# Windowed attention with the values made once per token, masks in 32-row tiles, and attention outputs brought back by plain transposes

## The reference, cut to what matters

```python
mod = (silu(c) @ wmod).reshape(8, 6, 1, -1)        # sa, ca, ga, sb, cb, gb per sequence
h = layernorm(x) * (1 + ca) + sa
q, k, v = split(h @ w_qkv)                         # 16 heads of 8 columns
# windows of W = 64 tokens: a query sees its own window up to itself, and the whole window before
kcat, vcat = concat([k_prev, k_cur]), concat([v_prev, v_cur])   # 128 keys; window 0 has no k_prev
attn = softmax(where(causal & valid, q @ kcat.T / 8 ** 0.5, -inf))
x = x + ga * ((attn @ vcat) @ w_out)
h = layernorm(x) * (1 + cb) + sb
# 8 experts of 352 hidden columns, the best 2 per token, weights by a softmax over both scores
x = x + gb * moe(h)
```

## Time and profile before

| | |
|---|---|
| median of 3 executions | 282.27 us (280.81, 282.27, 283.45) |
| the profiled execution's own time | 282.76 us |
| its span, first to last instruction | 280.7 us |
| mean granted TensorE clock | 0.92 of full speed |
| busy: PE, PEld, DVE, ACT, POOL | 221.5, 150.3, 171.0, 115.3, 128.6 us |
| stages in the span | loads and first scores to about 25 us, attention to about 147, experts to about 256, final sum to the end |

### The profile page before, as it was taken

One profiled execution on the slowest core, in us unless ns is written; L12 is line 12 of the kernel. 1 busy time (PEld: TensorE's weight loads), 2 busy tenths in 40 slices (PEclk: granted clock), 3 DMA queues, 4 the chain that ended last, 5 costly groups with the idle time before them and its releaser, 6 DMA issues.

```text
span 280.7 us, 7719 instructions
## 1 busy us (share of the span) xinstructions
PE 221.5 (79%) x2694; PEld 150.3 (54%) x2695; DVE 171.0 (61%) x527; ACT 115.3 (41%) x259; POOL 128.6 (46%) x127
## 2 busy tenths in 40 slices
PE   8559589998999999998867893877999999994000
PEld 3315245565756656574545572655777777773000
DVE  2665869899697685869491773624244444443492
ACT  4213255555546564545253441223444444443330
POOL 8450626251828557392505165714344444445251
PEclk9957799999999999999997999879999999999555
DMA  6479400000100000010102021222221111100751
GB/s 166 121 292 456 200 2 2 2 2 4 31 12 22 21 22 21 8 34 2 41 2 57 28 59 49 61 90 50 66 59 55 48 55 46 56 30 30 236 169 44
DMA packets 16488, 19.32 MB, mean 69 GB/s; under 512 B 2578, under 2 KB 14998, under 8 KB 16202
## 3 DMA queue, kind: packets, MB, share of 16 engines
q1 hardware_dynamic: 13786, 14.43, 16.4%
q0 software_dynamic: 2240, 4.28, 4.3%
q10 hardware_dynamic: 432, 0.20, 0.3%
HBM read 13.03 MB, written 6.13 MB: 68 GB/s over the span
## 4 chain that ended last, share of the span: by engine, by line
PE 58%; DVE 16%; ACT 7%; DMA 5%; issue 4%; POOL 4%; another core or an unknown queue 2%; SPq 1%; ACTq 0%; DVEq 0%; POOLq 0%
PE pair L742 8%; PE pair L716 7%; PE pair L718 7%; PE pair L557 6%; PE pair L501 4%; PE pair L536 4%; ACT pt L826 4%; PE pair L724 4%; DVE nd L996 3%; PE pair L542 3%; PE pair L572 2%; DVE fin_b L1314 2%; PE pair L474 2%; PE pair L735 2%
## 5 line engine op out<-in xcount | busy, mean ns | idle before, releaser
L1422 POOL DMA_INDIRECT ranked<-y_sb,ix_u x36 | 35.3, 980 | 47.4 <-ACT y_sb L916 36.8
L1290 DVE TENSOR_TENSOR gated<-pair,act 128x352 f32<-128x352 f32 x36 | 18.9, 525 | 51.5 <-PE pair L718 40.2
L826 ACT ACTIVATE pt<-pair 128x1024 f32<-128x1024 f32 x32 | 33.0, 1031 | 27.3 <-PE pair L542 27.3
L996 DVE TENSOR_REDUCE nd<-pair 128x8 f32<-128x1024 f32 x32 | 37.7, 1220 | 10.7 <-PE pair L501 10.7
L1375 POOL DMA_INDIRECT routed<-pay,row_u x32 | 32.2, 1005 | 13.7 <-issue 6.3
L716 PE MATMUL pair<-we_sb,x_t 128*128 x72 | 29.8, 497 | 3.1 <-ACT x_t L910 3.1
L742 PE MATMUL pair<-we_sb,gated_t 128*128 x216 | 31.6, 284 | 0.8 <-ACT y_sb L916 0.8
L742 PEld LDWEIGHTS pair<-we_sb,gated_t 128*128 128x128 f32 x216 | 27.9, 197 | 1.6 <-issue 1.2
L718 PE MATMUL pair<-we_sb,x_t 128*128 x72 | 28.3, 476 | 0.0
L1342 POOL TENSOR_TENSOR rstd<-veps,cf_sb 128x2 f32<-128x2 f32 x8 | 6.0, 748 | 46.8 <-DVE veps L1036 46.8
L501 PE MATMUL pair<-km,q_sb 32*64 32x512 f32 x256 | 20.5, 700 | 4.3 <-POOL km L1364 2.2
(11 more groups left out here) (164 smaller groups left out, 399.9 us busy)
## 6 DMA issues: line engine op xcount, KB each, us to landing
we_sb<-we SPq DMA_DIRECT2D x1, 4352.0 KB, 18.6
xt_in<-routed SPq DMA_DIRECT2D x36, 64.5 KB
mod_bc<-mod_rows SPq DMA_DIRECT2D x1, 2048.0 KB, 7.8
fin_y<-ranked SPq DMA_DIRECT2D x8, 256.0 KB, 4.5
out<-fin_b SPq DMA_DIRECT2D x8, 128.0 KB, 1.8
x_all<-x SPq DMA_DIRECT2D x1, 896.0 KB, 6.8
ranked<-y_sb,ix_u POOLq DMA_INDIRECT x36
routed<-pay,row_u POOLq DMA_INDIRECT x32
```

What stands on the lines that cost most here:

```text
L826: act.activation(pt[:, 2 * half:2 * half + 2, :].rearrange("p j k -> p (j k)"), src[:, :], ACT.Exp).then_inc(done, 1)
L996: dve.tensor_reduce(nd[:, :, 2 * half:2 * half + 2, 0].rearrange("p s j -> p j s"), src[:, :].rearrange("p (j s k) -> p j s k", j=2, s=4), ...
L1290: dve.tensor_tensor(gated[n][:, 0:HID], H3_BANK[n][:, 0:HID], act1[n][:, :], ALU.mult).then_inc(gated_ready, 1)
L1422: pool.indirect_dma_start(ranked[:, :], bass.IndirectOffsetOnAxis(ap=ix_u[q][:, 0:1], axis=0), y_sb[q][:, :], None, bounds_check=TOPK * TO ...
```

## The change

- `project_v` makes V once per token: two matmuls of 128 tokens, 256 columns of M1. h_t loses its 64 zero columns and their memset. `copy_v` copies V in three pieces: all 128 rows of a tile to the odd chunk; rows 0 to 63 to the even chunk, as current keys; rows 64 to 127 of tile 0 to chunk 2, as previous keys.
- So in even chunks the current keys stand first, on partitions 0 to 63, and the previous ones on 64 to 127. In `scores_t` the even chunk's matmul is split into two of 64 output rows. POOL zeroes the ones of chunk 0 on partitions 64 to 127.
- The masks come from a small tile `late32` (the triangle's first 32 rows over 64 columns, and rows 32 to 63 over the last 32 columns), held four times, for each group of 32 partitions; 8 small DMAs load it, ahead of the large load of x. In `scores` 16 mask matmuls with 32x32 tiles take the place of 8; in `scores_t` 8 with 32x64 and 8 with 32x32 tiles, of 128 columns each, take the place of 4, now for both chunks apart.
- `output_t` makes four plain transposes, 512 columns of M0; `perm_o` goes, with its wait and its two POOL copies. `divide_output` picks outputs and denominators by its access pattern, with as many elements as before.
- `gate` moves ahead of `project_v`, and into M1 behind V (column 272; Z1 for the leftover period). DVE reads its scores by `read_gate` ahead of `divide_output`. New waits: `read_gate` for `v_copied` (the bank is read by ACT too) and for `hot1_ready` of the batch before; `neg_max_t` in period0, and the expert stage's step 2, for `sc8_ready`.

```diff
@@ sync
             sp.dma_start(cb_sb[:, :], cb[:, 0:CB_USED]).then_inc(ld_b, 16)
+            la = CB["late"][0]
+            for j in range(4):
+                sp.dma_start(late32[32 * j:32 * j + 32, 0:W], cb[0:32, la:la + W]).then_inc(ld_b, 16)
+                sp.dma_start(late32[32 * j:32 * j + 32, W:W + 32], cb[32:64, la + 32:la + W]).then_inc(ld_b, 16)
             sp.dma_start(x_all[:, 2:NT, :], xv[:, 2:NT, :]).then_inc(ld_x, 16)
@@ tensor, project_v
-                for c in range(4):
-                    last = mm(M1[:, c * P:(c + 1) * P], h_t[:, c * W:c * W + 2 * W], wqkv_sb[:, 2 * D:3 * D],
+                for t in range(2):
+                    last = mm(M1[:, t * P:(t + 1) * P], h_t[:, t * P:(t + 1) * P], wqkv_sb[:, 2 * D:3 * D],
                               start=True, stop=True)
@@ scores
-                for n in range(2):
-                    for a in range(2):
-                        for i in range(2):
-                            sv = S_BANKS[2 * i + n].rearrange("p (s k) -> p s k", s=4)
-                            mm(half(sv, a)[:, :, W:2 * W], half(ident_b, i)[:, 64 * i:64 * i + 64],
-                               half(late, i).unsqueeze(1).to_broadcast([W, 4, W]), start=True, stop=False,
-                               skip_group_check=True)
+                late = late32[:, 0:W].unsqueeze(1).to_broadcast([P, 4, W])
+                later = late32[:, W:W + 32].unsqueeze(1).to_broadcast([P, 4, 32])
+                for a in range(2):
+                    for j in range(4):
+                        sv = S_BANKS[j].rearrange("p (s k) -> p s k", s=4)
+                        one = group(ident_b, j)[:, 32 * j:32 * j + 32]
+                        mm(sv[64 * a:64 * a + 32, :, W:2 * W], one, group(late, j), start=True, stop=False,
+                           skip_group_check=True)
+                        mm(sv[64 * a + 32:64 * a + 64, :, W + 32:2 * W], one, group(later, j), start=True, stop=False,
+                           skip_group_check=True)
@@ scores_t
                     for j in range(4):
-                        fv = F_BANKS[j].rearrange("p (s q) -> p s q", s=4)
-                        mm(fv[:, :, a * W:(a + 1) * W], group(k_sb[par], j)[:, c * W:c * W + 2 * W],
-                           group(qm[par], j)[:, :, c * W:(c + 1) * W], start=False, stop=False, skip_group_check=True)
-                for n in range(2):
-                    for i in range(2):
-                        fv = F_BANKS[2 * i + n].rearrange("p (s q) -> p s q", s=8)
-                        one = half(ident_b, i)[:, 64 * i:64 * i + 64].unsqueeze(1).to_broadcast([W, 8, W])
-                        last = mm(half(fv, 1), half(late, i), one, start=False, stop=True, skip_group_check=True)
+                        fv = F_BANKS[j].rearrange("p (s q) -> p s q", s=4)[:, :, a * W:(a + 1) * W]
+                        for low, keys in ((0, 2 * W),) if a else ((0, W), (W, W)):
+                            at = c * W + (W - low if a == 0 else 0)
+                            mm(fv[low:low + keys], group(k_sb[par], j)[:, at:at + keys],
+                               group(qm[par], j)[:, :, c * W:(c + 1) * W], start=False, stop=False,
+                               skip_group_check=True)
+                for a in range(2):
+                    for j in range(4):
+                        one = group(ident_b, j)[:, 32 * j:32 * j + 32].unsqueeze(1).to_broadcast([32, 4, 32])
+                        fv = F_BANKS[j].rearrange("p (s q) -> p s q", s=4)[:, :, a * W:(a + 1) * W]
+                        mm(fv[64 * a:64 * a + 64, :, 0:32], group(late32, j)[:, 0:W], one, start=False, stop=False,
+                           skip_group_check=True)
+                for a in range(2):
+                    for j in range(4):
...
+                        last = mm(fv[64 * a + 32:64 * a + 64, :, 32:64], group(late32, j)[:, W:W + 32], one,
+                                  start=False, stop=True, skip_group_check=True)
@@ output_t
-                        at = (2 * p + r) * RCOLS
-                        last = mm(M0[:, at:at + RCOLS], o_sb[:, p, r, :], perm_o[:, :], start=True, stop=True,
-                                  skip_group_check=True)
+                        at = (2 * p + r) * P
+                        last = pe.transpose(M0[:, at:at + P], o_sb[:, p, r, :], ident)
@@ tensor, period0
+                if b < B:
+                    pe.wait_ge(negt_ready, 2 * b + 1)
+                if b >= 2:
+                    gate(b - 2, M1 if b < B else Z1)
                 if b + 1 < B:
-                    pe.wait_ge(negt_ready, 2 * b + 1)
                     project_v()
...
-                    gate(b - 2, M0)
...
+                    if b >= 2:
+                        pe.wait_ge(sc8_ready, b - 1)
                     neg_max_t(2 * b + 1)
@@ scalar, copy_v
-                act.copy(v_lane[b % 2][:, :, HD:2 * HD],
-                         M1.rearrange("p (h e) -> p h e", e=HD)).then_inc(v_copied, 1)
+                to = v_lane[b % 2][:, :, HD:2 * HD].rearrange("p (t n h) e -> p t n h e", t=2, n=2)
+                v = M1[:, 0:2 * P].rearrange("p (t h e) -> p t h e", t=2, e=HD)
+                act.copy(to[:, :, 1, :, :], v)
+                act.copy(to[0:W, :, 0, :, :], v[0:W])
+                act.copy(to[W:2 * W, 1, 0, :, :], v[W:2 * W, 0, :, :]).then_inc(v_copied, 1)
@@ vector
-                rv = M0[:, 0:4 * RCOLS].rearrange("p (x c) -> p x c", c=RCOLS)
-                dve.reciprocal(rden[:, :, :], rv[:, :, 64:RCOLS]).then_inc(sums_inverted, 1)
+                rv = M0.rearrange("p (x k d) -> p x k d", k=4, d=HD)
+                dve.reciprocal(rden[:, :, :], rv[:, :, 2:4, 0]).then_inc(sums_inverted, 1)
...
+            def read_gate(e, m):
                 dve.wait_ge(gate_done, e + 1)
+                if e + 4 <= B:
+                    dve.wait_ge(v_copied, e + 4)
+                if e >= 1:
+                    dve.wait_ge(hot1_ready, e)
                 dve.tensor_copy(sc8[:, :, :].rearrange("p a e -> p (a e)"),
                                 m[:, GATE_AT:GATE_AT + 2 * E]).then_inc(sc8_ready, 1)
...
@@ vector, period0
+                if b >= 2:
+                    read_gate(b - 2, M1 if b < B else Z1)
                 if b >= 1:
                     divide_output(b - 1)
                 if b >= 2:
-                    choose_experts(b - 2, M0)
+                    choose_experts(b - 2)
```

More of the change, by code:

```diff
@@ L40 @@
 G = 2 * B
-RCOLS = 72
 CF = {}
@@ L60 @@
 N_CB = _columns(CB, [("ident", P), ("before", P), ("ones", P), ("region", E), ("late", 4 * W), ("none", 4 * W)])
-CB_USED = CB["late"][0] + W
+CB_USED = CB["late"][0]
 def build(nc, x, c_t, wqkv, wout, wmod, wg_t, we, cf, cr, cb, out):
@@ L104, in build @@
         quadmask = sb("quadmask", [P, 4])
-        perm_o = sb("perm_o", [P, RCOLS])
         x_all = sb("x_all", [P, NT, D])
@@ L112, in build @@
         normed = sb("normed", [P, 2, D])
-        h_t = sb("h_t", [P, WIN])
+        h_t = sb("h_t", [P, S])
         q_sb = sb("q_sb", [P, S])
@@ L193, in build @@
         ones_b = cb_("ones")
-        late = cb_sb[:, CB["late"][0]:CB["late"][0] + W]
         nd_high = nd[:, :, :, :].rearrange("p s j i -> p (s j i)").bitcast(BF16).rearrange(
@@ L200, in group @@
             return t[32 * j:32 * j + 32]
-        def half(t, i):
-            return t[64 * i:64 * i + 64]
         def mod(b, which):
@@ L500, in scores @@
                     for j in range(4):
-                        last = mm(half(S_BANKS[j], a), group(q_sb, j)[:, c * W:c * W + W],
+                        last = mm(S_BANKS[j][64 * a:64 * a + 64, :], group(q_sb, j)[:, c * W:c * W + W],
                                   group(km[par], j)[:, :, c * W:c * W + 2 * W], start=False, stop=True,
@@ L803, in modulate @@
                     act.wait_ge(v_done, b)
-                act.activation(h_t[:, W:WIN], M0[:, 0:S], ACT.Identity, bias=mod_t[:, B + b:B + b + 1],
+                act.activation(h_t[:, :], M0[:, 0:S], ACT.Identity, bias=mod_t[:, B + b:B + b + 1],
                                scale=mod_t[:, b:b + 1]).then_inc(ht_ready, 1)
@@ L1256, in aside @@
                 if i == 5 and at == "b":
-                    choose_experts(B - 1, XT_BANK)
+                    read_gate(B - 1, XT_BANK)
+                    choose_experts(B - 1)
                 if i == 6:
```

35 lines of the change are left out of this document (15 added, 20 removed).

## The result

The changed kernel took **286.34 us** (median of four runs), the kernel before 282.61 us beside it (four): a ratio of **1.014, 95% interval 1.009 to 1.019**. The forecast was 280.3, its range ended at 284.2. The profiled execution has a span of 284.1 us against 280.7.

A forecast was written before the change was run, and what follows sets the result against it. PE's chain was taken to bound the kernel, with held PE signals setting negt's start in batches 3 to 6. Middle batches -1.96, batches 0 to 2 +0.33, last batch -0.34: sum -1.97, forecast 280.3 us, range 276.6 to 284.2.

The forecast's parts named there:

- V once: In project_v, two matmuls for four take four of eight passes off PE: 0.45 us less per batch.
- Transposes: In output_t, four transposed tiles take 0.44 us in place of 0.93: 0.48 less per batch.
- scores_t: Split product and new masks in scores_t: 1.74 us against 1.63, +0.11 for each of 16.
- two ends: Bounds for scores_t: -0.25 us if changing tile columns alone costs nothing, +0.5 if tiles don't run side by side or reloads add up.
- The middle batches, -1.96: Four batches that scatter while attending: negt follows the exponential unheld, -0.60, second scores_t +0.11; -0.49 us each.
- wrong from the root: Stated failure condition: output_t's two signals fall into a GpSimd issue's tail again, or x's load holds DVE over 0.3 us.
- Rival C: Middle batches gain nothing: the hold falls on whatever PE signals next, negt starts as before; +0.4, 282.7 us, chance 0.22.
- Rival B: Tile shape changes in scores_t cost more than 0.1 us each; at 0.5 per scores_t +3.35, 285.6 us, chance 0.13.
- DVE's way comes about 0.5 ahead: In middle batches ACT's exponential is late next; DVE's path to the second scores_t ends about 0.5 us before it.
- Batches 0 to 2: Saving worth nothing in batches 1 and 2, where DVE's stretched subtraction decides; three second scores_t cost 0.11 each, +0.33 us.
- Rival A: Quicker scores masks let DVE beat GpSimd's product in batches 1 and 2, 0.8 to 0.9 off each; 278.6 us, chance 0.27.
- Start: Eight more SP DMAs delay x's large load by 3.8 us; nothing taken, 0.8 us if nothing covers it.

The follow-up runs named there:

- after_b: The changed kernel unaltered, run again beside the kernel before on a chip that held signals only 0.3 us: 277.20 us, ratio 1.003.
- the plain kernels: Changed kernel and kernel before, each with the 24 indirect scatters of batches 0 to 5 made plain transfers to fixed rows: 274.33 (ratio 0.993) and 273.11 us (0.991).
- m32fix2: Kernel before with the 32-row masks, their eight small loads and the two moves, on a chip that holds signals: 284.39 us, ratio 1.012.
- bfix2: Kernel before with the two moves alone, on a chip that holds signals: 282.85 us, ratio 1.007.
- two moves: Changed kernel with GpSimd's q product held back and VectorE's normalization put behind the next maximum: 271.08 us, ratio 0.983 on a quiet chip; 288.34, 1.029 on a holding one.
- sets 3 and 5: Two groups of follow-up kernels, each group on one chip that holds signals; the kernel before took 283.0 and 283.1 us there.
- sets 1, 2 and 4: Three groups of follow-up kernels, each group on one chip without long holds; the kernel before took 276.5, 277.5 and 274.6 us there.

## Why the prediction was wrong, step by step

- **V once:** -0.45 a batch; L471 to L531 is 0.62 us for 1.09 in the earlier trace rows: -0.47. **Transposes:** -0.48; 0.49 for 0.93: -0.44. **V copy** in three pieces, 0.9 us, hidden as said. **Masks** in `scores`: 0.26 for 0.34. These prices were right (0.93 over 8 passes is 0.116 and not 0.112, which changes nothing).
- **scores_t** was mis-sized: +0.11 forecast, 1.74 to 1.96 = **+0.22** measured. The working had 1.63 for the stage as it was, while the earlier trace rows give 1.74 from L531 to L604's start. For the new stage it counted 0.36 to the product, 1.06 for it and 0.32 for the masks; they are 0.33, 1.26 and 0.37. The splitting costs 0.40 alone, the new masks give 0.10 to 0.18 back. The prediction asked which of two ends holds for a change of columns alone: that of a cost.
- **The middle batches, -1.96: this is the step that failed, twice.** First, "ahead of the tail of the second indirect DMA, so the signal isn't held", and the exponential "starts at 108.19 as before". Both signals are held, for 1.8 us each (L551's from 109.23, L510's from 110.04), where the kernel before had 0.47 and 0.30, and batches 3 to 6 got 5.4 us longer. The prediction took the hold for one at the tail of an issue. The trace of before already had another one, in the second half of a batch, where the prediction saw none: L501's last row ends at 102.02, 0.5 us into an issue, and DVE starts on it only at 102.76, behind the end of that issue (PE, POOL and DVE of the kernel before):

```profile
100.91 1.11 PE L501 MATMUL pair<-km,q_sb 32*64 32x512 f32 x16
```
```profile
101.51 1.12 POOL L1375 DMA_INDIRECT routed<-pay,row_u  x1 [0.20 <-issue]
```
```profile
102.76 2.36 DVE L996 TENSOR_REDUCE nd<-pair 128x8 f32<-128x1024 f32 x2 [0.80 <-PE pair L501]
```

  The condition named as wrong from the root was met. Rival C had this cause, with "`negt` starts as before" as its worst, +0.4 in all: its price was the error. Rival B had the sign, for another reason.
- Second, and hidden by the first: "DVE's way comes about 0.5 ahead". On a chip without holds PE waits 0.96 us for DVE (after_b). DVE's rows had been read as they stood, not as they would lie against GpSimd's product once PE was earlier. Rows 7 showed just such a stretch, and I used it for batches 1 and 2 only.
- **Batches 0 to 2:** +0.33 forecast; batches 1 and 2 are 0.8 longer (0.6 also in after_b, against the trace of before on another chip), batch 0 shorter by a clock stretch. Rival A's gain didn't come. **Start:** 0.5 later, within 0 to 0.8, but not by the load of x: it is issued 3.7 us later and lands 5.3 us behind that, at 13.1, ahead of the statistics that read it (14.18). after_b started earlier than before did elsewhere, so where the 0.5 come from isn't settled. **Last batch:** nothing to tell from the clock's scatter.
- The net price of the change, -0.49 a middle batch, would have held within 0.13 (measured -0.36), had neither obstacle been there. That is luck in part: -0.60 of it was the end of a hold, and the plain kernels have no hold. By PE's own steps it would be -0.47 for V, -0.44 for the transposes and twice +0.22 for `scores_t`, -0.47.

**What stays open.** Why some chips hold PE's signals and others don't, and by what rule one is held and let go (some went near the end of the first issue of a pair, some within the second, most behind it). Why the change makes the holds longer: because PE signals at other moments, or because it has more small matmuls; no run separates the two, and m32fix2 shows that the masks alone are enough for much of it. What the kernel before does on a quiet chip in detail: all three profiles of the unaltered kernel fell on holding ones, and the batch of bfix2 and m32fix2 on a quiet chip wasn't measured. The half clock of 111.6 to 118.4 us follows the held signals, but no run separated its share, in the 3.3 us that this batch lost, from theirs.

## What to carry to other kernels

Measure what a shorter engine will wait for before counting its shortening: compare the other engines' chains as they will lie against GpSimd's work, not as they lie now. Where GpSimd runs elementwise products, put VectorE's PSUM reductions beside them, and its small SBUF copies and products elsewhere; here two moves gave 1.04 us in 16. Where GpSimd issues indirect transfers, look on more than one chip, and compare each signal's time with the end of its instruction. Issues 1.3 us or more apart held nothing here; whether spreading the pairs of the attention would free them wasn't tried.

## What the runs showed of the hardware that I had not expected

- On chips of the first measurement and of sets 3 and 5 completion signals of PE alone came up to 2.0 us late in the attention, and up to 4.7 in the expert stage, while GpSimd issued indirect DMAs one close behind another; beside plain issues, and beside indirect ones 1.3 us or more apart, none was late. On the chips of sets 1, 2 and 4 at most 1.6 us in sum over batches 3 to 6. The kernel before is at 281.4 to 283.1 on the former, 274.6 to 277.5 on the latter.
- One copy of four elements a partition took from 0.15 to 1.63 us, by where GpSimd's 1.9 us product stood; two reductions from PSUM 2.34 to 2.36 each time.
- Splitting 8 of 16 fp32 passes of 128 output rows into pairs of 64 cost 0.40 us, although the pieces use disjoint parts of the array.
